# Second attention interleaved with the experts' last units, and its softmax sums written by ScalarE's exponentials

## Chip, core and metric

One core of a Trainium2 chip. The metric is the device time of one execution in microseconds, the median of some runs; less is better.

## What is computed

Two transformer layers on x (4 x 256 rows of 256 columns, fp32), each with an attention and a feed-forward part. The change lies at the seam of the first layer's experts and the second layer's attention, and in that attention:

```
x = x + xattn0(ln(x), ctx)          # first attention
x = x + moe(ln(x))                  # 32 experts of width 96, top 8, rerouted
x = x + xattn1(ln(x), ctx, seg)     # second attention
x = x + ffn(ln(x))                  # 704 wide, silu(gate) * up, down

xattn1: kv_c = kv @ W_kvc;  q_c = q @ W_dq                # 64 and 96 columns
        q_nope = q_c @ W_uq (16 heads x 128);  q_rope = rope(q_c @ W_qr) (16 x 64)
        k_nope = kv_c @ W_uk;  v = kv_c @ W_uv;  k_rope = rope(kv_c @ W_kr)
        s = (q_nope . k_nope + q_rope . k_rope) / sqrt(192)
        s = s where seg-8 <= key <= seg, else -1e30       # 64 keys of the own batch
        p = softmax(s);  out = (p @ v) @ W_o
```

W_uq and W_uk are multiplied together ahead of time (absorb), as are W_uv and W_o (outmix, giving l_Bp) and the keys with the first product (keymix, giving l_KM).

## The kernel before

All tiles are placed by hand. Five engines run five instruction streams, with a semaphore for every hand-over. The eight PSUM banks are handed out ahead of time by class Banks: every product has a key, and `fill` waits until the bank's previous owner was read (`free`), `filled` until it is written (`full`). What is queued on TensorE is written out by the order functions: attention_order, moe_order and late_order; ScalarE, VectorE and GpSimd have loops of their own that follow them.

Experts. The 32 experts of width 96 are cut into 24 blocks of 128 columns (j) and two halves of 512 rows (h): 48 units, in the order of the list MOE, which goes through both halves of a block one behind the other, but for the last three blocks, where it takes all of half 0 and then all of half 1. A unit is gate_up (two banks of 512 columns, 12 matmuls), silu and the high part m_hh on ScalarE, the product with up, the routing weight and the low part m_hl on VectorE (times, split_h), and down (12 matmuls into the y banks 4 to 7), which runs two units behind gate_up. VectorE's settle adds y to x and does the layer norm of one half in small steps (ln_steps); 12 steps of half 0 are woven into each of the last two units, half 1 follows behind the last down.

Seam. Behind the last gate_up TensorE does outmix (four banks, read by ScalarE into l_Bp), the last two down, and keymix (eight banks, read into l_KM). Then late_order begins: for each pair of batches of 256 rows the transposes of x (turn, read into l_x2T), compress (q_c, read into l_qcT) and queries (the rope product of 16 heads, in four banks qr of a batch; parts 0 and 1 of a batch have two banks each). VectorE makes the mask l_mk from seg meanwhile.

A bank of queries takes three engines: ScalarE copies it with its halves of rows exchanged and one sign turned (swap_q), VectorE multiplies the bank by cos and the copy by sin (turn_q), GpSimd adds the two into QR (add_q), which lies in m_pre.

Chunks. The second attention then goes through eight chunks c of 128 rows, a loop over n on every engine. TensorE: scores2(c) into two banks, and two chunks later turn_p (8 transposes), values2 for a pair of chunks, project2 for a batch. VectorE: soft(c) (scale and mask out of PSUM into S, then the negative maximum), and scale(c) (sum, reciprocal, product). ScalarE: exps2(c), 16 Exp of 64 columns with the head's maximum as bias, and the copies of the transposes (l_PT) and of the values (l_x2T, reused). The dictionary QUERIES puts the remaining parts of queries into the first five chunks. add_l adds a batch's result to x and does its layer norm, then the FFN begins (f_turn, f_front, f_down). GpSimd prepares the FFN's weights between its adds (load_f).

Of the kernel before, what the change touches and what calls it, by code (L numbers as in the profile page):

```python
# [164 lines left out]
MOE = [(j, h) for j in range(21) for h in range(2)] + [(j, h) for h in range(2) for j in range(21, 24)]  # L165
# [7 lines left out]
def moe_order(do):  # L173
# [30 lines left out]
def late_order(do):  # L204

    for a, b in ((0, 1), (2, 3)):
        do("turn", a)
        do("turn", b)
        if a:
            do("queries", 1, 0)  # L210
        do("compress", a)
        do("compress", b)
        if a == 0:
            do("queries", 0, 0)
            do("queries", 0, 1)
    for n in range(12):
        if n < 8:
            do("scores", n)
        if n % 2 == 0 and n > 3:
            do("values", (n - 4) // 2)  # L220
        if 1 < n < 10:
            do("turn_p", n - 2)
        for m in QUERIES.get(n, ()):
            do("queries", m // 2, m % 2)
        if n % 2 and n > 4:
            do("project", (n - 5) // 2)
        if n % 2 and n > 6:
            do("f_turn", (n - 7) // 2)
        if n > 9:
            do("f_front", *FFN[n - 10])  # L230
# [36 lines left out]
def program(nc, A, out):  # L267
    ctx = ExitStack()
    with ctx:
# [120 lines left out]
        with c2:  # L390
# [5 lines left out]
            PT1 = sb("l_PT1", [128, 8, 256], F32, c2)  # L396
            dd = PT1[:, 0:2, :].rearrange("p a (b c) -> p (a b) c", b=4)
            qcT = sb("l_qcT", [96, 1024], F32, c2)
            S = [sb(f"l_S{i}", [128, 1024], F32, c2) for i in range(3)]
            s16 = [sb(f"l_s16{i}", [128, 2, 16], F32, c2) for i in range(3)]  # L400
            tqc = [prea[:, 8, :], prea[:, 9, :], S[0][:, 0:512], S[1][:, 0:512]] + [prea[:, 8 + n % 2, :] for n in range(12)]
            tqs = [prea[:, 12, :], prea[:, 13, :], S[0][:, 512:1024], S[1][:, 512:1024]] + [prea[:, 12 + n % 2, :] for n in range(12)]
# [3 lines left out]
            fhl = [sb(f"f_hl{i}", [128, 512], FR, c2) for i in range(3)]  # L406
        flat = lambda t: t[:].rearrange("p a b -> p (a b)")
# [18 lines left out]
        for key, b in ((("ln", 0), 3), (("ln", 1), 4), (("kx", 0), 5), (("vx", 0), 6), (("ln", 2), 7), (("ln", 3), 7)):  # L426
# [14 lines left out]
            "outmix": lambda: [("bp", z) for z in range(4)], "keymix": lambda: [("km", z) for z in range(8)]}), (0, 1, 2, 3))  # L441
# [5 lines left out]
        for bb in range(4):  # L447
            B.fill(("y", bb), 4 + bb, False)
        late = fills(late_order, {
            "turn": lambda bb: [("lt", bb)], "compress": lambda bb: [("qc", bb)],  # L450
            "queries": lambda bb, part: [("qr", bb, u) for u in range(2 * part, 2 * part + 2)],
# [3 lines left out]
        rest = [key for key in late if key[0] not in ("fg", "fu", "lo", "ft", "qr")]  # L455
        for key in late:
            if key[0] in ("lo", "ft"):
                B.fill(key, 6 + (key[0] == "lo" or key == ("ft", 3)))
            elif key[0] == "qr":
                B.fill(key, (6, 7, 2, 3)[key[2]] if key[1] == 0 else 6 + key[2] % 2)  # L460
            elif key[0] in ("fg", "fu"):
                B.fill(key, 2 * (FFN.index(key[1:]) % 2) + (key[0] == "fu"))
            else:
                B.fill(key, rest.index(key) % 6)
# [49 lines left out]
        added = count("added", units_q)  # L514
        swapped = count("swapped", [(bb, u) for bb in range(4) for u in range(4)])
        turned_q = count("turned_q", [(bb, u) for bb in range(4) for u in range(4)])
# [53 lines left out]
        def multiplied(key):  # L570
            c = multiplied_e if key in multiplied_e.at else multiplied_d
            return c.sem, c.at[key]

# [5 lines left out]
        def tensor(e):  # L579
# [278 lines left out]
            def outmix():  # L858
# [1741 lines left out]
```

## Time and profile before

| what | value |
| --- | --- |
| runs | 842.32, 845.23, 845.47 us (median 845.23) |
| profiled execution, first to last instruction | 841.8 us |
| TensorE busy | 782.3 us (93%) |
| VectorE busy | 663.8 us (79%) |
| ScalarE busy | 535.0 us (64%) |
| GpSimd busy | 469.1 us (56%) |
| last down of the experts ends | about 679.5 us |
| chunk loop of the second attention begins (scores of chunk 0) | 695.9 us |
| first FFN product begins | 781.4 us |

The profiled execution is one of its own; the page gives its span and nothing around it, so it stands 3.4 us under the median of the runs. A matmul's span in the trace is its way through a pipeline: for TensorE the distance from one start to the next is the cost, and not the duration of one. An fp32 matmul stands as two records. L997 is the line of the helper by which ScalarE makes its copies, so its rows are told apart by the tile.

### The profile page before, as it was taken

The page shows a single profiled execution, that of the slowest core. Times are in us where ns is not written, and L with a number is a line of the kernel's source. Part 1 is how long each engine was busy: PE and PEld are TensorE (multiplying, and loading weights), DVE is VectorE, ACT ScalarE, POOL GpSimd, SP SyncE. Part 2 cuts the span into 40 slices and gives each one's busy share as a digit, 9 for nine tenths or more (in the row PEclk, how much of TensorE's full clock was granted, in tenths as well). Part 3 has the DMA queues.
Part 4 walks back from the last instruction along what each step waited for, and adds up shares of the span by engine and source line. Part 5 has one row for each costly group of instructions (what it writes and reads, how often), then busy time and mean ns, then how long its engine had stood idle before and what let it go on. Part 6 is the DMA issues. An engine that isn't in the chain of part 4 may idle for free.

```text
span 841.8 us, 14343 instructions
## 1 busy us (share of the span) xinstructions
PE 782.3 (93%) x4848; PEld 670.3 (80%) x4848; DVE 663.8 (79%) x1563; ACT 535.0 (64%) x1236; POOL 469.1 (56%) x786
## 2 busy tenths in 40 slices
PE   3687999999999999999899999999999999798998
PEld 2566788888888888888788878998888877577787
DVE  7789899899998989979889794865654589976634
ACT  6788877787778877788664555433332268974332
POOL 3688969779686895858855676442210015980000
PEclk9699999999999999999999999999999999999999
DMA  7000120011200121000200323967421010100001
GB/s 242 14 0 1 39 76 1 2 39 39 76 1 1 39 66 48 2 2 1 68 26 14 127 64 98 243 167 249 133 63 51 1 45 14 51 14 0 1 1 51
DMA packets 28265, 45.59 MB, mean 54 GB/s; under 512 B 3937, under 2 KB 18081, under 8 KB 28065
## 3 DMA queue, kind: packets, MB, share of 16 engines
q1 hardware_dynamic: 26800, 41.31, 17.0%
q10 hardware_dynamic: 1392, 3.37, 1.1%
q8 instruction: 39, 0.64, 0.3%
q14 instruction: 34, 0.27, 0.1%
HBM read 43.49 MB, written 1.18 MB: 53 GB/s over the span
## 4 chain that ended last, share of the span: by engine, by line
PE 59%; DVE 22%; ACT 11%; issue 5%; DMA 2%; POOL 1%; SPq 1%; ACTq 0%; DVEq 0%
PE PS L772 16%; PE PS L842 8%; PE PS L632 6%; PE PS L727 4%; PE PS L701 4%; PE PS L663 4%; PE PS L953 2%; PE PS L684 2%; PE PS L654 2%; PE PS L673 2%; DVE st L1638 2%; DVE yb L1540 2%; ACT P L1111 1%; PE PS L711 1%; DMA l_KM<-share 1%
## 5 line engine op out<-in xcount | busy, mean ns | idle before, releaser
L2222 POOL TENSOR_SCALAR raw<-raw,mvq,rsq 128x128 f32<-128x128 f32 x312 | 182.9, 600 | 1.6
L772 PE MATMUL PS<-xq,WH 128*128 128x512 f32 x472 | 148.5, 396 | 1.0 <-ACT l_x2T L997 1.0
L772 PEld LDWEIGHTS PS<-xq,WH 128*128 128x128 f32 x472 | 86.3, 190 | 18.1 <-issue 2.1
L632 PE MATMUL PS<-WH,xq 128*128 128x256 f32 (+1 forms) x256 | 88.7, 366 | 8.1 <-DVE xq L1544 8.1
L772 PE MATMUL PS<-xq,WL 128*128 128x512 f32 x236 | 92.5, 392 | 0.0
L632 PE MATMUL PS<-WL,xq 128*128 128x256 f32 (+1 forms) x256 | 84.5, 349 | 0.0
L1111 ACT ACTIVATE P<-PS,sm 128x256 f32<-128x256 f32 x128 | 61.0, 497 | 25.7 <-DVE sm L1702 25.6
L842 PE MATMUL PS<-xq,m_hh 128*128 128x256 f32 x384 | 69.9, 283 | 2.5 <-DVE m_hl L1998 1.2
L1638 DVE BATCH_NORM_STATS2 st<-raw 128x6 f32<-128x128 f32 x320 | 70.6, 277 | 1.5 <-ACT raw L1083 1.5
L701 PE MATMUL PS<-PT,vr 128*128 128x256 f32 x256 | 66.5, 382 | 4.7 <-ACT PT L997 4.7
L663 PE MATMUL PS<-kT,qT 128*128 128x256 f32 x256 | 65.9, 380 | 1.8 <-ACT qT L1100 1.8
L842 PEld LDWEIGHTS PS<-xq,m_hh 128*128 128x128 f32 x384 | 60.8, 189 | 6.1 <-issue 2.8
L727 PE MATMUL PS<-PH,cat 128*128 128x256 f32 x256 | 64.6, 292 | 0.3 <-DVE cat L1544 0.2
L2352 POOL TENSOR_TENSOR m_pre<-m_pre 128x512 f32<-128x512 f32 x14 | 18.5, 1331 | 78.0 <-DVE m_pre L2063 78.0
L632 PEld LDWEIGHTS PS<-WH,xq 128*128 128x128 f32 x256 | 50.2, 196 | 14.2 <-issue 8.1
L1083 ACT ACTIVATE raw<-PS,sca 128x512 f32<-128x512 f32 (+1 forms) x96 | 57.5, 648 | 6.2 <-PE PS L632 4.8
L727 PE MATMUL PS<-PL,cat 128*128 128x256 f32 x256 | 61.5, 280 | 0.0
L1353 ACT ACTIVATE m_sg<-PS 128x512 f32<-128x512 f32 x28 | 16.7, 597 | 70.4 <-PE PS L772 70.4
L1985 DVE TENSOR_TENSOR m_sg<-m_sg,PS 128x512 f32<-128x512 f32 x28 | 19.2, 687 | 49.5 <-PE PS L772 49.5
L654 PE MATMUL PS<-idf,raw 128*128 128x128 f32 x320 | 48.6, 275 | 7.2 <-ACT yT L1147 2.4
L632 PEld LDWEIGHTS PS<-WL,xq 128*128 128x128 f32 x256 | 50.5, 197 | 4.8
L842 PE MATMUL PS<-xq,m_hl 128*128 128x256 f32 x192 | 54.0, 281 | 0.0
(301 smaller groups left out, 2177.7 us busy)
## 6 DMA issues: line engine op xcount, KB each, us to landing
wst<-in_wgu SPq DMA_DIRECT2D x24, 256.0 KB, 4.0
l_KM<-share SPq DMA_DIRECT2D x16, 384.0 KB, 3.9
wst<-in_wall SPq DMA_DIRECT2D x18, 256.0 KB, 3.1
l_KM<-share SPq DMA_DIRECT2D x16, 256.0 KB, 5.2
dst<-in_wdn SPq DMA_DIRECT2D x24, 128.0 KB, 3.4
wst<-in_wkvx SPq DMA_DIRECT2D x8, 256.0 KB, 3.3
l_KM<-share SPq DMA_DIRECT2D x16, 128.0 KB, 4.4
m_pre<-in_wo ACTq DMA_DIRECT2D x1, 2048.0 KB, 10.2
```

What stands on the lines that cost most here:

```text
L632: t = e.matmul(PS[:, b, o:o + n], xq[s][:, k, c * 128:(c + 1) * 128], W[:, k, w0:w0 + n], start=(k == 0 and i == 0), stop=(k == 1 and i == 1))
L654: t = e.transpose(PS[:, b, o:o + 128], raw[:, (2 * s + ci) % 4, h * 128:(h + 1) * 128], idf[:, :])
L663: t = e.matmul(PS[:, b, c * 256:(c + 1) * 256], qT[s % 2][:, k, c * 128:(c + 1) * 128], kT[s % 2][:, k // 2, :], start=True, stop=True)
L701: t = e.matmul(PS[:, b, 0:256], vr[:, (2 * s + tc) % 8, k // 2 * 128:(k // 2 + 1) * 128], PT[(5 * s + k) % 4][:, tc, :], start=(tc == 0), ...
L727: t = e.matmul(PS[:, b, c * 256:(c + 1) * 256], cat[:, j, c * 128:(c + 1) * 128], W[:, j, :], start=(j == 0 and W is PH and c == 0), stop= ...
L772: t = e.matmul(PS[:, b, :], W[wi][:, gu, k, :], a[:, k, cols], start=(n == 0), stop=(n == 5))
L842: t = e.matmul(PS[:, 4 + ch // 2, ch % 2 * 256:ch % 2 * 256 + 256], a[:, cc * 128:(cc + 1) * 128], D[wi], start=(first and p == 0 and ch % ...
L1083: t = e.activation(dst, PS[:, b, o:o + n], ACT.Copy, scale=sca[:, sc:sc + 1])
L1111: t = e.activation(P_[:, c, :], PS[:, b, c * 256:(c + 1) * 256], ACT.Exp, bias=m[:, 0, c:c + 1], accum_out=m[:, 1, c:c + 1])
L1638: e.bn_stats(st6[:, o + h, :], raw[:, n % 4, h * 128:(h + 1) * 128]).then_inc(dv.sem, 1)
L1985: e.tensor_tensor(src, src, PS[:, b, :], ALU.mult).then_inc(free[b], 1)
L2222: t = e.tensor_scalar(v, v, mvq[:, par, n, 0:1], rsq[:, par, n:n + 1], ALU.add, ALU.mult)
```

## The change

MOE turns to the order by halves at block 20 and no more at 21. The seam is taken apart: outmix, turn, compress, keymix and queries are issued by bank or pair, the transposes and compress of batches 0 and 1 and batch 0's queries between and behind the last two down, now in banks 4 and 5 in turn. ScalarE's copies follow the new order. VectorE makes the mask in units 26 to 31 of the experts, gives 7 steps of settle to each of the last three units, and adds the rotated queries of batch 0 itself; GpSimd adds those of batches 1 to 3. In the chunk loop values stands ahead of scores, transposes 7 behind project 2, add_l 1 ahead of the scaling of chunk 7, and all banks are fixed by a table. The 16 Exp of a chunk get an accumulator output each (accum_out into s16), and the TENSOR_REDUCE that made the sums is gone. Some tiles of the last stages are placed anew, so that those needed early do not lie over the experts' own. The loads of seg and f_sc are issued in the middle of the experts.

```diff
-MOE = [(j, h) for j in range(21) for h in range(2)] + [(j, h) for h in range(2) for j in range(21, 24)]
+MOE = [(j, h) for j in range(20) for h in range(2)] + [(j, h) for h in range(2) for j in range(20, 24)]
@@ moe_order
-    for n in range(2, len(MOE) + 2):
-        if n < len(MOE) and MOE[n][0] >= NPRE:
-            do("gate_up", *MOE[n])
-        if n == len(MOE):
-            do("outmix")
-        if n >= 2:
-            do("down", *MOE[n - 2])
-    do("keymix")
+    for n in range(2, len(MOE)):
+        if MOE[n][0] >= NPRE:
+            do("gate_up", *MOE[n])
+        do("down", *MOE[n - 2])
+    do("down", *MOE[-2])
+    do("outmix", 0)
+    do("outmix", 1)
+    do("down", *MOE[-1])
+    do("outmix", 2)
+    do("turn", 0)
+    do("turn", 1)
+    do("outmix", 3)
+    do("compress", 0)
+    do("compress", 1)
+    do("keymix", 0)
+    do("queries", 0, 0)
+    do("keymix", 1)
+    do("queries", 0, 1)
+    do("keymix", 2)
+    do("keymix", 3)
-QUERIES = {0: (3,), 1: (4,), 2: (5,), 3: (6,), 4: (7,)}
+QUERIES = {1: (4,), 2: (5,), 3: (6,), 4: (7,)}
@@ late_order
-    for a, b in ((0, 1), (2, 3)):
...
+    do("queries", 1, 0)
+    do("turn", 2)
+    do("turn", 3)
     for n in range(12):
+        if n % 2 == 0 and n > 3:
+            do("values", (n - 4) // 2)
         if n < 8:
             do("scores", n)
-        if n % 2 == 0 and n > 3:
-            do("values", (n - 4) // 2)
-        if 1 < n < 10:
+        if n == 0:
+            do("queries", 1, 1)
+            do("compress", 2)
+            do("compress", 3)
+        if 1 < n < 9:
             do("turn_p", n - 2)
         for m in QUERIES.get(n, ()):
             do("queries", m // 2, m % 2)
         if n % 2 and n > 4:
             do("project", (n - 5) // 2)
+        if n == 9:
+            do("turn_p", 7)
@@ banks
+        B.ring(fills(moe_order, turned), (4, 5))
+        home = {
+            "lt": lambda bb: bb, "qc": lambda bb: bb, "qr": lambda bb, u: 6 + u % 2, "lo": lambda bb: 7,
+            "ft": lambda bb: 6 + (bb == 3), "ls": lambda c, z: 4 * (c % 2) + z, "lp": lambda c, z: 2 * (c < 6) + z,
+            "lv": lambda bb, z: 2 + z, "fg": lambda j, h: 2 * (FFN.index((j, h)) % 2),
+            "fu": lambda j, h: 2 * (FFN.index((j, h)) % 2) + 1}
@@ scalar: exps2, and the order of the copies
                 for h in range(16):
                     s1 = S[c % 3][:, h * 64:(h + 1) * 64]
-                    t = e.activation(s1, s1, ACT.Exp, bias=s16[c % 3][:, 0, h:h + 1])
+                    t = e.activation(s1, s1, ACT.Exp, bias=s16[c % 3][:, 0, h:h + 1],
+                                     accum_out=s16[c % 3][:, 1, h:h + 1])
...
+            take_bp(0)
+            take_bp(1)
+            take_bp(2)
+            take_lt(0)
+            take_lt(1)
+            take_bp(3)
+            take_qc(0)
+            take_qc(1)
+            take_km(0)
+            swap_q(0, 0)
+            take_km(1)
+            swap_q(0, 1)
+            take_km(2)
+            take_km(3)
+            swap_q(1, 0)
+            take_lt(2)
+            take_lt(3)
@@ vector: turn_q adds batch 0 itself; settle; scale; add_l
+                        e.tensor_tensor(QR[0][:, 2 * u:2 * u + 2, :].rearrange("p a b -> p (a b)"), tqc[n], tqs[n],
+                                        ALU.add).then_inc(added_d.sem, 1)
...
-                    for _ in range(12):
+                    for _ in range(7):
                         next(settling, None)
+                if 25 < n < 32:
+                    next(masking, None)
...
                 w.wait_ge(exped_l.sem, exped_l.at[c])
-                e.tensor_reduce(s16[i][:, 1, :], s3, X, ALU.add).then_inc(dv.sem, 1)
-                w.wait_ge(dv.sem, dv.up())
                 e.reciprocal(s16[i][:, 1, :], s16[i][:, 1, :]).then_inc(dv.sem, 1)
...
+                if n == 8:
+                    add_l(1)
...
-                if n in (6, 8, 10):
+                if n in (6, 10):
@@ sync
+            w.filled(("aw", 3))
+            e.dma_start(seg[:], A["seg"]).then_inc(seg_in, 16)
+            e.dma_start(fsc[:], A["fsc"]).then_inc(fsc_in, 16)
             for j in range(16, 24):
```

## Rows read from the trace of the kernel before

**Rows 1.** The page's first line.

```profile
span 841.8 us, 14343 instructions
```

**Rows 2.** Timeline of VectorE in an experts' unit: start, us, what, wait before it.

```profile
662.98 0.69 DVE L1985 TENSOR_TENSOR m_sg<-m_sg,PS 128x512 f32<-128x512 f32 x1 [2.15 <-PE PS L772]
```

**Rows 3.** Busy time by stage: length, PE, PEld, DVE, ACT, POOL, clock, DMA, GB/s.

```profile
701.10:739.50 38.40, 32.32 (x181) 23.96 (x181) 37.60 (x47) 35.74 (x105) 31.14 (x28) 0.96 0.13 35
739.50:771.00 31.50, 29.07 (x174) 22.21 (x173) 24.31 (x44) 21.54 (x72) 15.71 (x14) 1.00 0.04 9
711.45:720.26 8.81, 6.44 (x36) 4.89 (x36) 8.64 (x11) 8.71 (x29) 6.51 (x7) 1.00 0.10 37
```

**Rows 4.** Timeline of TensorE, start of the stage.

```profile
672.54 3.73 PE L865 MATMUL PS<-m_pre 128*64 128x256 f32 x32
...
687.49 3.62 PE L904 MATMUL PS<-l_qcT,m_pre 96*128 96x256 f32 x16
...
695.89 1.02 PE L915 MATMUL PS<-l_KM,l_qcT 96*128 96x512 f32 x2
...
699.40 1.89 PE L904 MATMUL PS<-l_qcT,m_pre 96*128 96x256 f32 x8
```

**Rows 5.** Timeline of TensorE, its waits and the projections.

```profile
720.39 1.09 PE L930 MATMUL PS<-idf,l_S 128*128 128x128 f32 x8 [2.37 <-DVE l_S L2091]
721.32 3.55 PE L904 MATMUL PS<-l_qcT,m_pre 96*128 96x256 f32 x8
...
732.43 1.16 PE L930 MATMUL PS<-idf,l_S 128*128 128x128 f32 x8 [2.15 <-DVE l_S L2075]
...
739.54 7.07 PE L953 MATMUL PS<-l_Bp,l_x2T 128*128 128x256 f32 x32
...
770.08 1.09 PE L930 MATMUL PS<-idf,l_S 128*128 128x128 f32 x8 [2.43 <-DVE l_S L2091]
771.01 7.07 PE L953 MATMUL PS<-l_Bp,l_x2T 128*128 128x256 f32 x32
...
781.35 0.70 PE L772 MATMUL PS<-xq,WH 128*128 128x512 f32 x2 [0.95 <-ACT l_x2T L997]
```

**Rows 6.** Busy time and granted clock in one microsecond.

```profile
722.00:723.00 1.00, 1.00 (x4) 0.73 (x4) 1.00 (x2) 1.00 (x4) 1.00 (x2) 0.50 0.00 0
```

**Rows 7.** Timeline of ScalarE in the chunks.

```profile
703.36 1.28 ACT L1394 ACT_TABLE_LOAD   x1
...
711.05 3.93 ACT L1394 ACTIVATE l_S<-l_S,l_s 128x64 f32<-128x64 f32 x16
714.89 1.05 ACT L997 ACTIVATE l_PT<-PS 128x512 f32<-128x512 f32 x2
...
718.40 3.93 ACT L1394 ACTIVATE l_S<-l_S,l_s 128x64 f32<-128x64 f32 x16
...
724.43 0.59 ACT L1426 ACTIVATE m_pre<-PS 64x512 f32<-64x512 f32 x1 [1.14 <-POOL m_pre L2352]
...
726.88 3.93 ACT L1394 ACTIVATE l_S<-l_S,l_s 128x64 f32<-128x64 f32 x16
```

**Rows 8.** Timeline of ScalarE in the first attention.

```profile
311.83 0.50 ACT L1083 ACTIVATE vr<-PS,sca 128x256 f32<-128x256 f32 x1
312.19 0.51 ACT L1111 ACTIVATE P<-PS,sm 128x256 f32<-128x256 f32 x1
312.54 0.24 ACT L1111 ACTIVATION_READ_ACCUMULATOR P<-PS,sm 128x1 f32 x1
312.64 0.51 ACT L1111 ACTIVATE P<-PS,sm 128x256 f32<-128x256 f32 x1
```

**Rows 9.** Timeline of VectorE, layer norm of half 1 and a sum.

```profile
679.68 1.29 DVE L2010 TENSOR_TENSOR xt<-PS,xt 128x512 f32<-128x512 f32 x2 [1.18 <-PE PS L842]
...
685.31 1.38 DVE L1519 TENSOR_SCALAR xn<-xt,mv,rs 128x256 f32<-128x256 f32 x4
...
717.13 1.21 DVE L2087 TENSOR_REDUCE l_s<-l_S 128x16 f32<-128x1024 f32 x1
```

More of the change, by code:

```diff
@@ L440, in program @@
             "gate_up": lambda j, h: [("g", j, h), ("u", j, h)],
-            "outmix": lambda: [("bp", z) for z in range(4)], "keymix": lambda: [("km", z) for z in range(8)]}), (0, 1, 2, 3))
+            "outmix": lambda z: [("bp", z)], "keymix": lambda y: [("km", 2 * y), ("km", 2 * y + 1)]}), (0, 1, 2, 3))
         B.ring(fills(moe_order, {
@@ L856, in down, with outmix @@
                 back(h, mhh[n % 3], mhl[n % 3], dn_of(j), j == 0, j == 23).then_inc(downed.sem, 1)
[L858 removed]
+            def outmix(z):
                 w.wait_ge(wo_in, 32)
[L860 to L867 removed]
@@ L869, in keymix @@
-            def keymix():
-                for y in range(4):
-                    banks = [fill(("km", 2 * y + o)) for o in range(2)]
-                    emptied(("aw", y))
-                    for i in range(2):
-                        for o, b in enumerate(banks):
-                            rows = slice(64 * o, 64 * o + 64)
-                            t = e.matmul(PS[0:96, b, i * 256:(i + 1) * 256], AT[rows, 2 * y + i, :], KA[rows, :],
-                                         start=True, stop=True)
-                            if i:
-                                t.then_inc(full[b], 1)
@@ L881, in tensor @@
-            experts = {"early": early, "xs": xs, "logits": logits, "absorb": absorb, "turn_oh": turn_oh, "rows": rows,
-                       "turn_cw": turn_cw, "gate_up": early, "down": down, "outmix": outmix, "keymix": keymix}
-            moe_order(lambda kind, *a: experts[kind](*a))
+                b = fill(("bp", z))
+                for o in range(2):
+                    for p in (2 * z, 2 * z + 1):
+                        h = 2 * p + (o ^ (z % 2))
+                        t = e.matmul(PS[64 * o:64 * o + 64, b, p % 2 * 256:p % 2 * 256 + 256], wuv[:, h, :],
+                                     wo[:, h, :], start=True, stop=True)
@@ new lines, in outmix, with keymix @@
+                t.then_inc(full[b], 1)
+            def keymix(y):
+                banks = [fill(("km", 2 * y + o)) for o in range(2)]
+                emptied(("aw", y))
+                for i in range(2):
+                    for o, b in enumerate(banks):
+                        rows = slice(64 * o, 64 * o + 64)
+                        t = e.matmul(PS[0:96, b, i * 256:(i + 1) * 256], AT[rows, 2 * y + i, :], KA[rows, :],
+                                     start=True, stop=True)
+                        if i:
+                            t.then_inc(full[b], 1)
@@ L906, in queries @@
                     t.then_inc(full[b], 1)
+            experts = {"early": early, "xs": xs, "logits": logits, "absorb": absorb, "turn_oh": turn_oh, "rows": rows,
+                       "turn_cw": turn_cw, "gate_up": early, "down": down, "outmix": outmix, "keymix": keymix,
+                       "turn": turn2, "compress": compress, "queries": queries}
+            moe_order(lambda kind, *a: experts[kind](*a))
             def scores2(c):
@@ L2107, in split_f @@
                                 xq[0][:, :, cols].bitcast(F32), ALU.subtract).then_inc(free[b], 1)
-            for part in range(3):
-                turn_q(part // 2, part % 2)
             def gate_f(n):
```

183 lines of the change are left out of this document (88 added, 95 removed).

## Prediction

> **What bounds the kernel now.** I read the page for the span [rows 1], then the timeline of the experts' last units, then busy time by stage, and looked for the stage in which no engine is full. The experts' last units are TensorE's: VectorE waits 2.15 us for it in each unit [rows 2]. The change touches what comes behind them, the second attention, which goes in eight chunks of 128 rows. From 701.1 to 739.5 us TensorE, VectorE and ScalarE are busy 32.3, 37.6 and 35.7 of 38.4 us: VectorE sets the pace and ScalarE is close behind; from 739.5 to 771.0 it is TensorE, 29.1 of 31.5 us [rows 3]. TensorE's timeline says the same: it waits 2.37, 2.15 and 2.43 us for VectorE's l_S and 0.95 us for ScalarE's l_x2T, and behind the first wait 8 records of queries take 3.55 us, where 16 took 3.62 [rows 4, 5], some 1.6 more. These 9.5 us are nearly all that the middle and the end of the stage can give back.
>
> **The change, part by part.**
>
> 1. Sums on ScalarE. Eight TENSOR_REDUCE of 1.21 us leave VectorE [rows 9], 1.25 us with the step between, 10 us in all. In exchange each of 128 Exp gets an accumulator. What that costs stands in the first attention, whose Exp has one: the ACTIVATION_READ_ACCUMULATOR begins 0.35 us behind its Exp and the next Exp 0.10 us behind the read, while the plain copy of the same width also takes 0.36 us from start to start [rows 8]. So the read adds 0.095 us; the rest of its 0.24 us is overlapped. The 64-column Exp goes at 3.84 us for 16 (711.05 to 714.89) [rows 7], 0.240 each; with a read 0.335, so 5.36 us for 16, 1.52 us more a chunk. Such a short Exp with a read is not in this trace; the bounds are 0 (the read fits where a short Exp leaves a gap) and 0.19 us (nearly nothing overlaps). I take 0.095, since it is the same pair of instructions, only wider.
> By the Trainium skill ("ScalarE: Activation LUTs", What ACT_TABLE_LOAD costs) an ACTIVATE with a pointer bias takes 280 ns + 0.833 ns a column, less 93 ns of overlap, and the row's 0.240 us agrees; it names no price for the read, and a sum that goes by it alone would have 0 in this place and end at a span of 835.0.
>
> 2. Who sets the pace then. In one chunk that still carries queries (711.45 to 720.26) VectorE is busy 8.64 and ScalarE 8.71 of 8.81 us [rows 3]. ScalarE's own work for such a chunk is 16 Exp 3.84, two l_PT copies 1.0, four swap copies 2.45 [rows 7]: 7.3 us, now 8.8. VectorE's 8.8 becomes 7.5. The exponentials came every 8.5 us (718.40, 726.88), and will come every 8.8: the bound moves over and the pace stays.
>
> 3. The start. Outmix, transposes, compress, keymix and the first queries are interleaved with the last down products, but it is the same TensorE work. Its pieces [rows 4]: outmix 0.92 a bank, a part of queries 1.73, scores 3.5; and by the records of the same stretch transposes 0.44, compress 0.88 and keymix 0.93 a call. Worked through in this profile's times: down 45 ends at 672.4; down 46 waits for VectorE until 673.3 and ends 674.8; two outmix 676.6; down 47 678.1; outmix 2, two transposes, outmix 3 680.8; two compress 682.5; keymix 0, queries, keymix 1 686.1. The second part of queries now has two banks instead of four. They are freed by VectorE, which first has its layer norm to do, 6.9 us behind down 47 (679.68 to 686.7 [rows 9], so 678.2 to 685.1), and then waits for ScalarE's swap: 1.5 us of waits, 689.4. Keymix 2, 3 691.3; queries (1,0) and transposes 693.9; scores 0 697.4, where it ended 699.4; queries (1,1), compress 2, 3 700.9, where the same work was done at 701.1. So TensorE is 0.2 us ahead and no more. ScalarE takes the last copy and begins its table load at 701.5, where it was 703.36 [rows 7]: 1.9 us ahead. In this lie the mask (moved under the experts, 2.4 us of VectorE) and the adds of the first batch (GpSimd's before, VectorE's now): VectorE is through with the fourth at 693.7, in time.
>
> 4. From there to the end. ScalarE has no gap: 701.5, table load 1.3, four chunks of 5.36, three parts of swaps 7.3, two pairs of l_PT 2.0, hand-overs 0.2: chunk 3's exponentials end at 733.7, where they ended at 730.8 (726.88 + 3.93). As differences: -1.9 start, -1.1 a wait for GpSimd (724.43 [rows 7]), +6.1 reads, -0.2 rounding, +2.9. Then TensorE in one piece: banks freed by two l_x2T copies 734.7, turn_p 2 0.9, queries 1.73, scores 5 3.5, turn_p 3 0.9: project 0 at 741.8, where it was 739.54 [rows 5], +2.3. From project 0 to project 2 it was 31.5 us. Now project 6.9, values 1.87, scores 3.5, turn_p 0.9, scores 3.5, turn_p 0.9, project 6.9, f_turn 0.5, values 1.87, turn_p 0.9, and 0.6 of waiting for ScalarE's values (its chunk 7 ends at 767.8, the copies at 770.1): 28.4 us, -3.1. Transposes 7 stand behind project 2 now, so their wait of 2.43 us is gone with them. Behind project 2 their 0.9 us and 0.2 us for their copy come in, the 0.95 us ahead of the first FFN unit go: 0. The sum +2.3 - 3.1 = -0.8: span 841.8 - 0.8 = 841.0.
>
> 5. What I cost at nothing. The order of experts 20 to 23 and the first layer norm begun a unit earlier: seven steps in unit 45 are 3.0 us against 2.15 of cover [rows 2], 0.9 us late, and the split has 1.1 us more to spare; uncovered, each microsecond would be TensorE's. The mask's five steps of 0.2 to 0.7 us have the same cover. f_sc and seg stand ahead of expert 16's weights on SP: two short issues whose wait passed long before; gu and dn behind them are staged many units ahead. add_l 1 ahead of scale 7: VectorE is through at 773, TensorE asks at 777. Values ahead of scores 4 makes TensorE wait from 721.1 to 726.0 for ScalarE's copy of transposes 1, but that wait ends before the one on chunk 3.
>
> **Rivals.**
> The read is cheap. At 0 the +6.1 of four chunks are gone, the tail stays TensorE's: 835.0. For it: a short Exp has idle lanes behind it, 0.240 us for 64 columns against 0.36 for 256. Against: the 0.10 us in the pair.
> The read is dear (slower). ScalarE is on the path in chunks 0 to 3, 6 and 7, 96 reads, so 0.01 us of read is 0.96 us of time: at 0.19 us the span is 841.0 + 9.1 = 850.1. It decides from 0.15 us. For it: the read's own 0.24 us.
> The clock. At 722 to 723 us the granted clock is 0.50, the 1.2 GHz level [rows 6], behind a wait of 2.37 us, and cost 1.6 us. My schedule has a wait of 3.4 us ahead of the chain to project 0: +1.6 if the clock falls there, +3.2 if twice: 842.6 to 844.2. Against: behind the waits of 2.15 and 2.43 us the records kept their pace.
> The Trainium skill ("TensorE: Matmul & The Clock Gate", Part 1) says that half rate is the default and sustained work lifts it; by that rule this rival is the likely one, and the trace agrees at one of three waits.
>
> **How the numbers follow.** The three runs have a median of 845.23, 3.4 over the profiled span; I keep that: 841.0 + 3.4 = 844.4. The sum as worked out 0.46, the clock 0.14 (846.0 to 847.6), a cheap read or a better start 0.20 (838.4 to 841), a dear read or new waits at the start 0.20 (849.5 to 853.5). 0.5% is 4.2 us, about what a measurement of this kernel can tell from no change; the bounds are 841.0 and 849.5. So faster 0.20, same 0.60, slower 0.20. The range takes the first two with 2 us of error of such a hand schedule and about half of each of the others: 839.0 to 850.5.
>
> **What would show it.** 16 Exp with reads in 5.3 to 5.5 us; the table load at 700.5 to 702.5; TensorE waiting for ScalarE and no longer for VectorE's l_S between 717 and 735 us; project 0 later than 739.5, project 2 a little before 771.0; VectorE's row 10 us less. Wrong it would be by a pair of Exp and read under 0.29 or over 0.39 us, a table load before 700, experts' units longer than before, or a wait for queries' banks of over 2 us about 687.

## The result and the profile after

The changed kernel takes 848.84 us in the median (846.33 to 850.97, 8 runs) against 845.25 (842.32 to 847.0, 8 runs) before: ratio 1.0046, 95% interval [1.0031, 1.0061]. By the ratio that is slower by 3.9 us (3.6 between the medians), where I had forecast 0.8 us faster. The profiled execution of the changed kernel spans 844.5 us and took 846.33, so 1.8 us lie around its span, where I had carried 3.4. Of the kernel's 8 runs it is the fastest, so its span stands 4.3 us under their median.

The page after, its head ([rows 1] before):

```profile
span 844.5 us, 14474 instructions
...
PE 784.3 (93%) x4848; PEld 668.6 (79%) x4848; DVE 656.2 (78%) x1559; ACT 546.8 (65%) x1364; POOL 459.2 (54%) x782
```

VectorE has 7.6 us less (663.8 before) and ScalarE 11.8 us more (535.0 before), which is 128 reads of 0.092 us.

Busy time by stage, columns as in [rows 3]; the first stage begins in down 45 and ends 0.7 us ahead of scores of chunk 1, the second ends at project 0, the third at project 2:

```profile
670.20:700.90 30.70, 28.81 (x182) 21.15 (x181) 25.22 (x62) 18.89 (x34) 2.54 (x2) 1.00 0.00 1
700.90:742.20 41.30, 35.01 (x185) 24.27 (x184) 31.92 (x41) 40.84 (x173) 29.95 (x28) 0.88 0.14 39
742.20:773.60 31.40, 28.14 (x166) 21.10 (x164) 17.89 (x38) 26.68 (x132) 13.22 (x13) 1.00 0.00 1
```

In the second row ScalarE (the fourth figure behind the length) is busy 40.84 of 41.30 us: it is the bound now, and VectorE, the bound of [rows 3], has 9 us to spare. In the third no engine is full, so the engines wait for one another there.

TensorE's timeline after: its waits in the chunks and the projections ([rows 5] before):

```profile
718.83 1.09 PE L946 MATMUL PS<-idf,l_S 128*128 128x128 f32 x8 [1.79 <-DVE l_S L2139]
719.93 3.29 PE L915 MATMUL PS<-l_qcT,m_pre 96*128 96x256 f32 x8
726.82 3.69 PE L956 MATMUL PS<-l_PT,l_BDK 64*64 64x512 f32 x16 [3.59 <-ACT l_PT L1013]
...
735.18 1.06 PE L946 MATMUL PS<-idf,l_S 128*128 128x128 f32 x8 [0.78 <-ACT l_x2T L1013]
...
742.18 7.07 PE L969 MATMUL PS<-l_Bp,l_x2T 128*128 128x256 f32 x32
...
773.63 7.15 PE L969 MATMUL PS<-l_Bp,l_x2T 128*128 128x256 f32 x32 [3.29 <-ACT l_x2T L1013]
```

The wait for the scaled probabilities of chunk 7, 2.43 us before, is gone, and in its place project 2 (773.63) waits 3.29 us for ScalarE's copy of the values. Project 0 begins 2.6 us later than the 739.54 of [rows 5], and project 2 no nearer to it: 31.45 us instead of 31.47.

Each stretch of TensorE's program, from these starts and the same ones before:

| stretch (us) | before | forecast | after |
| --- | --- | --- | --- |
| end of down 45 | 672.4 | 672.4 | 671.6 |
| to scores of chunk 1 | 28.7 | 28.5 | 30.0 |
| to project 0 | 38.4 | 40.9 | 40.6 |
| to project 2 | 31.5 | 28.4 | 31.45 |
| to project 3 | 13.2 | 13.2 | 13.6 |
| to the end | 57.6 | 57.6 | 57.3 |

The differences after less before are -0.8, +1.3, +2.2, 0, +0.4, -0.3: the 2.7 us of the spans within rounding. Three rows miss the forecast by more than half a microsecond: the end of down 45 (-0.8), the start (+1.5) and project 0 to project 2 (+3.05). The spans differ by 1.2 us less than the ratio says, and that part I can't place.

### The profile page after: what moved, and what is told of

Same layout as the page of the kernel before. It is cut to its first block, busy times and chain, and to the rows that moved or that the text cites. A ratio compares the mean times of both kernels' runs of the same rounds, so it can differ in the third digit from the quotient of the medians.

```text
span 844.5 us, 14474 instructions
## 1 busy us (share of the span) xinstructions
PE 784.3 (93%) x4848; PEld 668.6 (79%) x4848; DVE 656.2 (78%) x1559; ACT 546.8 (65%) x1364; POOL 459.2 (54%) x782
## 4 chain that ended last, share of the span: by engine, by line
PE 60%; DVE 20%; ACT 13%; issue 4%; DMA 2%; POOL 1%; ACTq 0%; SPq 0%; DVEq 0%; POOLq 0%
PE PS L789 18%; PE PS L859 8%; PE PS L649 6%; PE PS L744 4%; PE PS L718 3%; PE PS L680 3%; ACT l_S L1397 3%; PE PS L969 2%; DVE st L1665 2%; PE PS L701 2%; PE PS L690 2%; PE PS L671 2%; DVE yb L1567 2%; ACT P L1127 2%; DVE cat L1571 1%
## 5 line engine op out<-in xcount | busy, mean ns | idle before, releaser
L2402 POOL TENSOR_TENSOR m_pre<-m_pre 128x512 f32<-128x512 f32 x12 | 15.6, 1308 | 88.0 <-DVE m_pre L2078 88.0
L1099 ACT ACTIVATE raw<-PS,sca 128x512 f32<-128x512 f32 (+1 forms) x96 | 57.6, 648 | 5.9 <-PE PS L649 4.4
```

Source lines behind the costliest of these rows:

```text
L1099: t = e.activation(dst, PS[:, b, o:o + n], ACT.Copy, scale=sca[:, sc:sc + 1])
```

## Experiments

My theory after the comparison had four parts. The read costs what I said, and all of it is paid in the chunks that ScalarE bounds. The 3.1 us of the tail were kept back by VectorE's order: add_l(0), the addition and layer norm of batch 0, stands ahead of soft(7), the scale and maximum of chunk 7, and ScalarE can't begin the exponentials of chunk 7 before. The start loses what it loses by the many turns from one product to another and by waits for two banks. And TensorE's clock costs nothing where TensorE waits for another engine anyway. The rival was my forecast's own one: that new waits of the early start, not the reads, make it slower.

All kernels in one table. Ratios are against the kernel before on the same chip in the same batch. The three distances are of the profiled execution, in us, on TensorE's timeline but for the table load, which is ScalarE's last act before the exponentials. The first distance can be compared only within one order of the start (in the new one outmix begins behind down 46). One profiled execution stands behind each row of distances; the start of the first outmix alone lies between 673.2 and 677.3 us in the kernels with the new order.

| kernel | ratio, 95% interval | first outmix to scores 0 | table load to project 0 | project 0 to 2 |
| --- | --- | --- | --- | --- |
| before | 1 | 23.35 | 36.2 | 31.5 |
| after | 1.0046 [1.0031, 1.0061] | 20.41 | 39.9 | 31.45 |
| e1_sums_vector | 0.9987 [0.9973, 1.0001] | 20.41 | 35.3 | 31.3 |
| e2_old_order_reads | 1.0015 [0.9998, 1.0032] | 23.33 | 38.5 | 30.8 |
| e3_norm_later | 1.0016 [0.9999, 1.0033] | 20.41 | 39.9 | 30.7 |
| e4_no_sums | 0.9962 [0.9944, 0.998] | 20.41 | 34.9 | 30.7 |
| e6_vector_norm_split | 0.9959 [0.9943, 0.9974] | 20.41 | 35.4 | 29.2 |
| e7_reads_norm_split | 0.9995 [0.9977, 1.0014] | 20.41 | 39.9 | 29.0 |
| e8_reads_first_four | 1.0033 [1.0019, 1.0046] | 20.41 | 39.9 | 31.2 |
| e9_start_grouped | one run | 23.08 | 39.9 | 31.45 |
| e10_old_start_new_tail | 0.998 [0.9959, 1.0001] | 23.36 | 37.8 | 28.5 |
| e11_keymix_first | 0.9958 [0.9939, 0.9977] | 19.87 | 35.3 | 29.3 |
| e12_sums_shared | 0.998 [0.9961, 0.9998] | 19.87 | 36.95 | 29.2 |

**e1: the change without the reads.** The sums go back to VectorE, everything else stays.

```diff
-                    t = e.activation(s1, s1, ACT.Exp, bias=s16[c % 3][:, 0, h:h + 1],
-                                     accum_out=s16[c % 3][:, 1, h:h + 1])
+                    t = e.activation(s1, s1, ACT.Exp, bias=s16[c % 3][:, 0, h:h + 1])
@@ scale
+                e.tensor_reduce(s16[i][:, 1, :], s3, X, ALU.add).then_inc(dv.sem, 1)
+                w.wait_ge(dv.sem, dv.up())
```

> The changed kernel with the softmax sums back as VectorE's TENSOR_REDUCE; the new order of the start is kept. Theory A (the 128 accumulator reads put ScalarE on the path of chunks 0 to 3 and of chunks 6 and 7): table load stays near 702.3 us, project 0 at 738 to 739 us instead of 742.2, project 2 at 767.5 to 770 instead of 773.6, time 843.5 to 845.5, no slower than the kernel before. Theory B (the loss is the start, cut into small pieces on TensorE, and the order of the chunks): project 0 not before 741 and the time within 1 us of the changed kernel, 848 to 849.

Measured: 844.19 us, ratio 0.9987, against the 1.0046 of the change as made. The new order is worth a little, the reads cost 0.6% of the time, 5 us. From the table load to project 0 it is 35.3 us, so 4.6 of the 5 us are in chunks 0 to 3. The wait ahead of project 2 stays without the reads, and so is not theirs; ScalarE stands still for VectorE's maximum of chunk 7. TensorE's timeline of e1, its wait ahead of project 2, then ScalarE's, the exponentials of chunk 7:

```profile
769.79 0.45 PE L969 MATMUL PS<-l_Bp,l_x2T 128*128 128x256 f32 x1 [2.45 <-ACT l_x2T L1013]
```

```profile
763.31 3.93 ACT L1397 ACTIVATE l_S<-l_S,l_s 128x64 f32<-128x64 f32 x16 [5.12 <-DVE l_s L2130]
```

**e2: the reads without the change.** The kernel before with the two edits of e1 the other way round.

> The kernel before with only the sums moved to ScalarE (accumulator outputs in, TENSOR_REDUCE out). Theory A: ScalarE's exponentials of chunk 3 end 4 to 5 us later than the 730.8 us of before, project 0 at 743 to 744.5 instead of 739.5, time 848.5 to 850.5. Theory B: VectorE is relieved and the time is within 1 us of the kernel before, 844 to 846.

Measured: 846.89 us, ratio 1.0015, between the two theories. In the old order the same 128 reads cost 1.3 us and not 5, at the edge of what the interval tells from nothing. From the table load to project 0 they cost 2.3 us (36.2 to 38.5). The exponentials of the four chunks begin at the same pace in both orders: 704.37, 712.25, 721.09, 729.93 in e2, and 703.59, 711.47, 720.30, 729.14 after. What differs comes behind: from the start of chunk 3's exponentials to project 0 it is 11.6 us in e2 and 13.0 after. TensorE's timeline of e2, transposes of chunk 2 and what follows:

```profile
732.16 1.61 PE L930 MATMUL PS<-idf,l_S 128*128 128x128 f32 x8 [2.65 <-DVE l_S L2076]
733.56 3.16 PE L904 MATMUL PS<-l_qcT,m_pre 96*128 96x256 f32 x8
```

In the old order these transposes follow scores of chunk 4 in banks 2 and 3. They wait until VectorE's scaling and masking of chunk 4 has read them (L2076 of e2 is that line, and so is the L2075 of the 2.15 us in [rows 5]), and begin 2.2 us behind the start of chunk 3's exponentials. After, they wait for ScalarE's l_x2T (735.18 above) and begin 6.0 us behind it: the new bank table gives banks 2 and 3 to the values just before, and the copies that free them are queued behind 16 exponentials of 5.3 us. That these shared banks are the whole of the 1.4 us is argued from the rows and not shown; no kernel with another table was run.

**e3: add_l(0) wholly behind soft(7).**

```diff
                 if n < 8:
                     soft(n)
-                if n == 8:
-                    add_l(1)
+                if n in (7, 8):
+                    add_l(n - 7)
...
-                if n in (6, 10):
-                    add_l((n - 6) // 2)
+                if n == 10:
+                    add_l(2)
```

> The changed kernel with one thing moved on VectorE: the add and layer norm of batch 0 (4.8 us) go from ahead of chunk 7's maximum to behind it. If the 3.3 us that TensorE waits for ScalarE's values ahead of project 2 are this norm, through the late start of chunk 7's exponentials: these start 2.4 us earlier, the wait falls to 0.6 to 1.0 us, time 845.5 to 847. If they are ScalarE's own work (reads, and a copy for the FFN ahead of the values): the wait stays over 2.5 us and the time 848 to 849.

Measured: 846.25 us, ratio 1.0016. TensorE's timeline of e3, project 1 and project 2:

```profile
761.70 7.17 PE L969 MATMUL PS<-l_Bp,l_x2T 128*128 128x256 f32 x32 [1.83 <-DVE xt L2145]
...
772.63 1.75 PE L969 MATMUL PS<-l_Bp,l_x2T 128*128 128x256 f32 x7 [0.42 <-ACT l_x2T L1013]
```

The wait ahead of project 2 falls from 3.29 to 0.42 us as expected, and 1.83 us come up ahead of project 1, which needs the bank that the addition in add_l(0) reads. Net 0.8 us between the projections; the ratio fell by 2.5 us against the change as made, and the rest lies within the two intervals. The addition has to stay early, and only the layer norm may go late.

**e4: no sums at all.** The reads are gone, nothing takes their place, and VectorE's reciprocal reads the maxima, so this kernel leaves out the normalisation.

```diff
-                                     accum_out=s16[c % 3][:, 1, h:h + 1])
@@ scale
-                e.reciprocal(s16[i][:, 1, :], s16[i][:, 1, :]).then_inc(dv.sem, 1)
+                e.reciprocal(s16[i][:, 1, :], s16[i][:, 0, :]).then_inc(dv.sem, 1)
```

> The changed kernel without softmax sums on any engine: the reciprocal is taken of the maxima instead, so the probabilities are not normalised; nothing else is left out. It shows what is left when neither ScalarE nor VectorE pays. Theory A: project 0 at 735.5 to 737.5 us, time 840.5 to 843. Theory B: project 0 not before 740, time over 846.

Measured: 842.05 us, ratio 0.9962. Project 0 came at 737.95 us, a little behind the expected 737.5. This is what the sums cost altogether, by the ratios: 2.1 us on VectorE (e1), 7.1 on ScalarE (after). With no sums on any engine project 2 still waits 2.46 us for l_x2T, so that wait has nothing to do with where sums are made.

**e6: e1, with add_l(0) split.** The addition stays at unit 6, the layer norm goes behind soft(7).

```diff
-            def add_l(bb):
+            def add_x(bb):
...
+            def norm_l(bb):
                 w.emptied(("lo", bb))
                 w.emptied(("qc", bb))
                 weave(ln_steps(bb, 1, xn_f.sem))
+
+            def add_l(bb):
+                add_x(bb)
+                norm_l(bb)
...
                 if n < 8:
                     soft(n)
+                if n == 7:
+                    norm_l(0)
...
-                if n in (6, 10):
-                    add_l((n - 6) // 2)
+                if n == 6:
+                    add_x(0)
+                if n == 10:
+                    add_l(2)
```

> Sums on VectorE, new order of the start, and on VectorE only the add of batch 0 stays ahead of chunk 7's maximum (0.7 us, it frees project's bank), its layer norm goes behind it. If the norm is what holds up chunk 7's exponentials (ScalarE waits 5.1 us for them in the kernel with sums on VectorE) and through them project 2 (2.45 us): project 2 follows project 1 at 10.6 to 11.2 us behind its end's transposes and values without a wait over 0.5 us, and the time falls by 2 to 2.5 us against that kernel, to 841.5 to 843 us, below the kernel before. If it is not: within 0.7 us of 844.2.

Measured: 841.57 us, ratio 0.9959 [0.9943, 0.9974]. TensorE's timeline of e6, projects 1 and 2, and VectorE's, addition, scale and maximum of chunk 7, then the norm:

```profile
755.93 7.07 PE L969 MATMUL PS<-l_Bp,l_x2T 128*128 128x256 f32 x32
...
766.76 1.53 PE L969 MATMUL PS<-l_Bp,l_x2T 128*128 128x256 f32 x6 [0.42 <-ACT l_x2T L1013]
```

```profile
754.87 0.68 DVE L2146 TENSOR_TENSOR xt<-PS,xt 128x512 f32<-128x512 f32 x1
755.47 1.28 DVE L2124 SCALAR_TENSOR_TENSOR l_S<-PS,l_mk 128x512 f32<-128x512 f32 x2
756.85 1.22 DVE L2130 TENSOR_REDUCE l_s<-l_S 128x16 f32<-128x1024 f32 x1
757.99 0.74 DVE L1530 BATCH_NORM_STATS2 st<-xt 128x6 f32<-128x256 f32 x2
```

The wait ahead of project 1 is not there and 0.42 us are left ahead of project 2, project 0 to project 2 takes 29.2 us, and this is, level with e11, the fastest kernel of the study that makes the sums. Only the place of the layer norm differs from e1, and the time is 2.4 us less.

**e7: the change as made, with the same split.**

> The changed kernel with its reads on ScalarE and the same split of batch 0's norm. The wait ahead of project 2 (3.3 us) falls under 0.8 us and no wait for the project bank comes in its place (1.8 us where the whole add was moved): time 845.3 to 846.3. Then 4.6 us of reads still stand between it and the twin with sums on VectorE (3 to 4.5 us slower than that one). Rival: ScalarE with its reads in chunks 6 and 7 is late by itself, the wait stays over 2 us and the time over 847.

Measured: 844.89 us, ratio 0.9995, a little under the expected time; the wait ahead of project 2 is 0.81 us. Against the 1.0046 of the change that is 4.3 us less, of which the profile places 2.5 between project 0 and project 2 (31.45 to 28.96); the rest lies within the two intervals, and I can't place it. Against e6 the reads cost 0.36%, 3 us. Its profiled span of 845.1 us is long because its experts ended 3 us later in that execution (first outmix at 677.26, where it was 674.21 after); I use its distances only.

**e8: reads in chunks 0 to 3 only.** Chunks 4 to 7 have their sums on VectorE.

```diff
-                                     accum_out=s16[c % 3][:, 1, h:h + 1])
+                                     accum_out=s16[c % 3][:, 1, h:h + 1] if c < 4 else None)
@@ scale
+                if c > 3:
+                    e.tensor_reduce(s16[i][:, 1, :], s3, X, ALU.add).then_inc(dv.sem, 1)
+                    w.wait_ge(dv.sem, dv.up())
```

> The changed kernel with reads in chunks 0 to 3 only and VectorE's TENSOR_REDUCE in chunks 4 to 7. If the price of the reads is paid wholly where queries are still being swapped (chunks 0 to 3, 4 x 1.5 us): the time is that of the changed kernel, 848 to 849.5. If reads in chunks 6 and 7 count too, as the forecast's 96 reads had it: 845.5 to 847.

Measured: 848.08 us, ratio 1.0033, against 1.0046 with all reads and 0.9987 with none. The reads of chunks 0 to 3 carry nearly the whole loss; those of chunks 4 to 7 cost 1.1 us, inside the intervals. The 96 reads that my rival of a dear read put on the path were by this little more than the 64 of chunks 0 to 3.

**e9: the start with fewer turns.** Outmix 2 and 3 together, keymix 0 and 1 together, queries (0,0) and (0,1) together, ScalarE's copy of outmix 3 moved with it.

```diff
     do("outmix", 2)
+    do("outmix", 3)
     do("turn", 0)
     do("turn", 1)
-    do("outmix", 3)
     do("compress", 0)
     do("compress", 1)
     do("keymix", 0)
-    do("queries", 0, 0)
     do("keymix", 1)
+    do("queries", 0, 0)
     do("queries", 0, 1)
```

> The changed kernel with the start on TensorE in larger groups: outmix 2 and 3 together, keymix 0 and 1 together, the two parts of batch 0's queries together. In the changed kernel 22.0 us lie between the start of the last-but-one down and scores of chunk 0, where the pieces at their old cost give 20.9. If each turn from one product to the next costs 0.1 us: 21.4 to 21.7 us, less what waits for banks take. If it is the waits alone: 22.0 or more.

Measured: one run, 849.54 us; first outmix to scores 0 is 23.08 us, 2.7 us longer. TensorE's timeline of after first, then of e9, from the first keymix:

```profile
682.71 1.11 PE L891 MATMUL PS<-l_KA,l_AT 64*96 64x256 f32 x8
683.75 1.99 PE L915 MATMUL PS<-l_qcT,m_pre 96*128 96x256 f32 x8
685.67 1.11 PE L891 MATMUL PS<-l_KA,l_AT 64*96 64x256 f32 x8
687.02 1.13 PE L915 MATMUL PS<-l_qcT,m_pre 96*128 96x256 f32 x4 [0.24 <-DVE l_S L2077]
688.95 1.13 PE L915 MATMUL PS<-l_qcT,m_pre 96*128 96x256 f32 x4 [0.79 <-DVE l_S L2077]
690.01 1.97 PE L891 MATMUL PS<-l_KA,l_AT 64*96 64x256 f32 x16
```

```profile
681.86 1.97 PE L891 MATMUL PS<-l_KA,l_AT 64*96 64x256 f32 x16
683.77 1.99 PE L915 MATMUL PS<-l_qcT,m_pre 96*128 96x256 f32 x8
687.00 1.13 PE L915 MATMUL PS<-l_qcT,m_pre 96*128 96x256 f32 x4 [1.24 <-DVE l_S L2077]
688.93 1.39 PE L915 MATMUL PS<-l_qcT,m_pre 96*128 96x256 f32 x4 [0.80 <-DVE l_S L2077]
690.25 3.35 PE L891 MATMUL PS<-l_KA,l_AT 64*96 64x256 f32 x16
```

Two keymix in a row take 1.91 us from start to start (681.86 to 683.77), where one that another product follows takes 1.04 (682.71 to 683.75 after): a turn costs 0.1 to 0.2 us. But the first queries now stand behind both keymix and begin 10.61 us behind the first outmix, where it was 9.54. Their banks come free as much later, so the next queries begin 13.84 us behind it and not 12.81, with waits of 1.24 and 0.80 us ahead of them; and behind these the same two keymix take 3.35 us instead of 1.97. Busy time and granted clock of e9 in that stretch:

```profile
690.00:692.00 2.00, 2.00 (x9) 1.26 (x10) 1.97 (x4) 1.18 (x2) 0.00 (x0) 0.50 0.00 0
692.00:694.00 2.00, 2.00 (x12) 1.27 (x9) 1.97 (x4) 1.45 (x3) 0.00 (x0) 0.73 0.00 0
```

0.50 is the 1.2 GHz level. So the 2.7 us are 1.0 of later queries, 1.4 of the fall and 0.3 that I don't place, and the expectation of a gain failed. In this execution the clock fell once more, in project 2 behind its wait of 3.30 us, which cost another 1.6 us.

**e10: the new tail on the old start.** Only transposes 7 behind project 2, add_l(1) ahead of chunk 7's scale, and the split of e6, in the kernel before.

```diff
-        if 1 < n < 10:
+        if 1 < n < 9:
             do("turn_p", n - 2)
...
             do("project", (n - 5) // 2)
+        if n == 9:
+            do("turn_p", 7)
...
```

> The kernel before with its start untouched (second attention's start behind the experts, sums on VectorE), and only the end of the second attention changed: the turn of chunk 7's probabilities behind project 2, the next normalisation ahead of chunk 7's scale, batch 0's add begun at unit 6 and its layer norm behind the softmax of chunk 7. Theory (the stall ahead of project 2 is VectorE's order and is worth its 2 us by itself): project 0 stays where it was, 67.0 us behind the first outmix, and project 0 to project 2 falls from 31.5 to about 29.2 us, so the time is 842.8 to 843.8, a ratio near 0.997. Rival (the gain of the kernel with both belongs to the early start): within 0.7 us of 845.3.

Measured: 843.09 us, ratio 0.998 [0.9959, 1.0001]. Project 0 to project 2 fell to 28.5 us, 2.9 less than before, so the theory of the tail holds. But in the profiled execution project 0 came 68.6 us behind the first outmix and not 67.0, which takes half of it back. TensorE's timeline of e10 around chunk 2's transposes, then its clock:

```profile
719.57 1.09 PE L932 MATMUL PS<-idf,l_S 128*128 128x128 f32 x8 [2.37 <-DVE l_S L2093]
720.50 2.00 PE L906 MATMUL PS<-l_qcT,m_pre 96*128 96x256 f32 x8
...
731.63 1.76 PE L932 MATMUL PS<-idf,l_S 128*128 128x128 f32 x8 [3.75 <-DVE l_S L2077]
733.18 2.92 PE L906 MATMUL PS<-l_qcT,m_pre 96*128 96x256 f32 x8
```

```profile
720.00:722.00 2.00, 2.00 (x14) 1.65 (x12) 2.00 (x4) 2.00 (x9) 1.92 (x2) 1.00 0.00 0
...
732.00:734.00 2.00, 2.00 (x9) 1.86 (x8) 1.90 (x3) 1.17 (x2) 2.00 (x3) 0.50 0.46 116
```

Set beside [rows 5]: there the clock fell [rows 6] behind the wait of 2.37 us, queries took 3.55, and the next wait was 2.15. Here, where TensorE's program is the same up to this point, it held behind the same wait, queries took 2.00, the 1.6 us saved went into the next wait (3.75), and behind that one the clock fell on the path: from chunk 2's transposes to project 0 it is 8.68 us instead of 7.11.

**e11: e6, with keymix 2 and 3 ahead of queries (0,1), and ScalarE's copies in the same order.**

```diff
-    do("queries", 0, 1)
     do("keymix", 2)
     do("keymix", 3)
+    do("queries", 0, 1)
```

> The kernel with sums on VectorE, the early start and the split normalisation, and the two last pieces of keymix now ahead of queries (0,1), with ScalarE's copies in the same order. Theory (queries (0,1) loses about 0.8 us in the waits for its bank, which keymix can cover): first scores 19.6 us behind the first outmix instead of 20.4, and 0.5 to 1 us less than the 841.6 of that kernel. Rival (VectorE's turn of the queries becomes what chunk 0 waits for, or the wait comes back ahead of the first scores): table load to project 0 grows from 35.4 to about 36.2 and the time stays within 0.3 us of 841.6.

Measured: 842.01 us, ratio 0.9958, where e6 has 0.9959: no difference. Scores 0 comes 0.54 us sooner behind the first outmix (keymix 3 now waits 0.97 us for its bank), but the table load comes 28.34 us behind it where it was 28.09: ahead of it ScalarE waits 1.70 us for VectorE's and 0.30 and 0.70 us for GpSimd's part of the queries. That chain sets the time of chunk 0, and TensorE's gain ends in a wait. The rival had the wait and the missing gain right, though the wait is ahead of the table load and not behind it: from the table load to project 0 it is 35.3 us and not the 36.2 it named.

**e12: sums shared.** e11, with the sums of heads 0 to 7 of chunks 0 to 3 read by ScalarE, all others reduced by VectorE. The edit is shown against e11.

```diff
-                    t = e.activation(s1, s1, ACT.Exp, bias=s16[c % 3][:, 0, h:h + 1])
+                    t = e.activation(s1, s1, ACT.Exp, bias=s16[c % 3][:, 0, h:h + 1],
+                                     accum_out=s16[c % 3][:, 1, h:h + 1] if c < 4 and h < 8 else None)
@@ scale
-                e.tensor_reduce(s16[i][:, 1, :], s3, X, ALU.add).then_inc(dv.sem, 1)
+                h0 = 8 if c < 4 else 0
+                e.tensor_reduce(s16[i][:, 1, h0:16], s3[:, h0:16, :], X, ALU.add).then_inc(dv.sem, 1)
```

> The kernel with keymix first, and in chunks 0 to 3 the sums shared: ScalarE keeps those of heads 0 to 7 by its accumulator, VectorE reduces heads 8 to 15; chunks 4 to 7 all on VectorE. Theory A (chunks 0 to 3 run at the pace of whichever of the two engines has more in a chunk, and all sums on ScalarE only pushed the larger load over to it): ScalarE pays 8 x 0.095 = 0.76 us a chunk, VectorE saves 0.6, the pace is about 8.0 us a chunk, table load to project 0 falls from 35.4 to 33.5 to 34 us, and the time is 1 to 2 us under that of the kernel with keymix first. Theory B (ScalarE alone sets the pace with its exponentials, copies and reads, and VectorE's sums lie beside it): every read is paid in full, 3 us over four chunks, table load to project 0 is 37.5 to 38.5, and the time is 2 to 3 us over it.

Measured: 843.7 us, ratio 0.998, 1.8 us over e11. The exponentials of chunks 0, 1 and 2 begin at 704.98, 712.12 and 720.22, in e11 at 704.52, 710.92 and 718.28: both distances are 0.74 us longer, eight reads of 0.093 us paid in full. Chunk 3's begin 8.10 us behind chunk 2's, in e11 8.33, and project 0 12.31 us behind those, in e11 11.92: the reads of chunks 2 and 3 cost 0.16 us together. Theory A fell: in chunks 0 and 1 ScalarE alone sets the pace. Theory B has the sign and half the size: of four chunks of reads the path paid for two.

## Why the forecast failed, step by step

The time of 848.84 us lies inside the range of 839.0 to 850.5 and within the half percent that I had called no change, but that was the width of the range and not the sum: the sum had a gain of 0.8 us, the ratio a loss of 3.9, and none of the rivals that made the range wide is what happened. The step that failed is the tail, between project 0 and project 2.

The cost of a read (part 1) was right. ScalarE's timeline after, beginning with the table load:

```profile
702.29 1.28 ACT L1397 ACT_TABLE_LOAD   x1
703.59 0.35 ACT L1397 ACTIVATE l_S<-l_S,l_s 128x64 f32<-128x64 f32 x1
703.84 0.19 ACT L1397 ACTIVATION_READ_ACCUMULATOR l_S<-l_S,l_s 128x1 f32 x1
703.93 0.33 ACT L1397 ACTIVATE l_S<-l_S,l_s 128x64 f32<-128x64 f32 x1
...
716.78 1.05 ACT L1013 ACTIVATE l_PT<-PS 128x512 f32<-128x512 f32 x2
```

A pair takes 0.333 us where I had 0.335, and 16 exponentials 5.31 us (711.47 to 716.78) where I had 5.36. The rivals of a cheap and of a dear read are both out; the read adds 0.093 us. What 64 of them cost on the path is less than their sum: I had 6.1 us less 1.1 of a wait for GpSimd, and e1 puts it at 4.6.

Who sets the pace (part 2). It did move over to ScalarE, and the 8.8 us a chunk are there: 711.47, 720.30, 729.14. "The pace stays" was loosely said, since without the reads only the last of the three distances is 8.5 us; the others are 7.35 (711.05 to 718.40 in [rows 7]) and 6.4 (from 704.66, a row not shown, to 711.05). The sum in part 4 didn't use that sentence: it had 32.2 us from the table load to the end of chunk 3's exponentials, and 32.17 were measured (702.29 to 734.46). One sign came out otherwise: TensorE still waited 1.79 us for VectorE's l_S at 718.83. VectorE had itself waited 0.69 us for ScalarE's exponentials ahead of it.

The start (part 3) was mis-sized. Down 45's end to scores of chunk 1: 28.5 forecast, 30.0 measured. I priced each piece of a product that was taken apart at its share of the whole (outmix 0.92 a bank, keymix 0.93 a call) and the rows show 1.02 and 1.04. Set against the forecast's own times, with 0.83 us added for the earlier end of the experts, the error grows from piece to piece to 1.4 us at the end of keymix 1 (forecast 686.1, measured 686.7 in an execution that is 0.8 us ahead) and then stays: ten turns from one product to another, 0.14 us each. The waits for queries' banks that I had at 1.5 us are 1.03 (0.24 and 0.79). The early start therefore gives ScalarE its table load 1.1 us earlier, of which the earlier end of the experts in this execution is 0.8, and not the 1.9 that I carried: ahead of it ScalarE waits 2.25 us for TensorE's queries (1,1), at 699.19.

To project 0 (part 4): 741.8 forecast, 742.18 measured, a late start and a slightly short chain together; the chain from the table load was 40.3 in the sum and is 39.9.

The tail (part 4) is the step that failed. I took the wait of 2.43 us ahead of chunk 7's transposes away, wrote 0.6 us of waiting for ScalarE's values, and had chunk 7's exponentials done at 767.8. They were done at 771.0. VectorE's and ScalarE's timelines after (765.67 is the first of the 16 exponentials):

```profile
758.23 0.68 DVE L2145 TENSOR_TENSOR xt<-PS,xt 128x512 f32<-128x512 f32 x1
...
763.03 1.28 DVE L2125 SCALAR_TENSOR_TENSOR l_S<-PS,l_mk 128x512 f32<-128x512 f32 x2
764.42 1.22 DVE L2131 TENSOR_REDUCE l_s<-l_S 128x16 f32<-128x1024 f32 x1
```

```profile
765.67 0.35 ACT L1397 ACTIVATE l_S<-l_S,l_s 128x64 f32<-128x64 f32 x1 [2.38 <-DVE l_s L2131]
...
770.99 0.57 ACT L1013 ACTIVATE xq<-PS 128x512 fp32r<-128x512 f32 x1
771.47 2.02 ACT L1013 ACTIVATE l_x2T<-PS 128x512 f32<-128x512 f32 x4
```

The scores of chunk 7 lay in their banks from about 759 on, but VectorE was 4.8 us in add_l(0) (758.23 to 763.03). So the exponentials began 2.38 us late, their copy followed at 771.47, and project 2 at 773.63. In the sum I had followed TensorE's own work and ScalarE's own work through this stretch, and not VectorE's, which is busy 24.3 of 31.5 us there [rows 3]; the prediction has no time for add_l(0) at all. The same order stood in the kernel before. ScalarE's timeline before, the exponentials of chunk 7:

```profile
762.22 3.93 ACT L1394 ACTIVATE l_S<-l_S,l_s 128x64 f32<-128x64 f32 x16 [3.22 <-DVE l_s L2081]
```

They were late then too: VectorE was in add_l(0) from 754.76 to 759.58 us, with the last scores of chunk 7 issued at 755.47. And transposes 7 behind them waited 2.43 us for chunk 7's scaled probabilities. Moving the transposes took away the wait that showed and left its cause. e3, e6, e7 and e10 show it by moving the layer norm (e3 the addition too, e10 on the old start): 30.7, 29.2, 29.0 and 28.5 us, against the 28.4 of the sum. e7 is the change as made but for that one move, and takes 2.5 of the 3.05 us back.

The clock. It did fall as that rival feared: 0.50 after the wait at 718.83, with values at 3.69 us where they take 1.95. It cost nothing, since TensorE waited for ScalarE on either side (3.59 and 0.78 us). The Trainium skill ("TensorE: Matmul & The Clock Gate", Part 1) has half rate as the default, and the trace agrees at this wait, but not at the 3.29 us ahead of project 2, where the granted clock stayed at 1.00. Whether a fall costs time is a second question, and my +1.6 us had taken it as answered. In e9 and e10 the fall was on the path and cost 1.4 and 1.6 us, the size that I had.

What I cost at nothing held as far as can be told: TensorE nowhere waited for the mask, for seg or for f_sc, and down 45 ended between 670.6 and 674.7 us in the ten profiled kernels with the new order (672.2 in the mean), between 671.6 and 672.5 in the three with the old one, so some tenths more can't be excluded. VectorE's row fell by 7.6 us and not by the 10 that I named as a sign: the four adds of batch 0 of 0.69 us each that came over from GpSimd were in part 3 and not in that sentence.

Taken together: the reads cost 5.0 us in the new order by e1 and 3.0 by e7 against e6, where the traces have 4.7 and 4.3, and 1.3 in the old order. The new order without them gains 1.1 us, at the edge of its interval; e6 against e10, which has the old start and bank order with the same tail, gives 1.8, also not clear of noise. The 2.4 us of the tail (e6 against e1) were to be had by moving one layer norm, which neither kernel does. Open stay the 1.8 us of e7 and 1.7 of e3 that no stretch shows, and how much of the 1.4 us behind chunk 3 the shared banks carry.

## What to carry to other kernels

A sum over a short row by ScalarE's accumulator cost 0.09 to 0.10 us an instruction here, behind 64 columns and behind 256; sixteen of them outweigh one reduction of 1.2 us, and pay only where ScalarE has the time free. When a wait is taken away, follow every engine through the stretch behind it, the idle ones first: a layer norm on an engine that is 57% busy held up the softmax of the last chunk. Cutting products into pieces to begin early cost 0.1 to 0.2 us a piece, and a bank shared between two uses ties the later use to the read that frees it, which may be queued behind long work.

## What the runs showed of the hardware

The read of the accumulator is an instruction of its own with 0.19 us on the record and 0.093 us on the path behind an Exp of 64 columns; in the first attention, behind 256 columns, 0.10 [rows 8]. The granted clock doesn't follow the length of the last wait alone: it held behind 2.37 us and fell behind 3.75 in e10, fell behind the same 2.37 us in the kernel before, behind 1.79 after, and behind 1.24 and 0.80 close together in e9. Ahead of project 2 it held behind 3.29 us after and fell behind 3.30 in e9, and held behind 2.45 in e1 and fell behind 2.46 in e4, each pair in the same order of TensorE's work. In the kernel before it fell at 721 us, off the path, and not again before project 0; in e10 it held there and fell at 732, on the path.
